# Causal attention of a decoder kernel: from the unit-pipelined stage with two score banks to the four-bank streamed stage

## What is computed

```python
n = layernorm(x[b])                         # no gain, no offset
q = n @ Wq; k = n @ Wk                      # Wq, Wk folded from a and b
v = n @ v_w.T + v_b
s = where(causal, q_h @ k_h.T, -inf) * 16 ** -0.5     # 16 heads, 112 x 112 each
x[b] += concat(softmax(s) @ v_h) @ o_w.T + o_b
```

## Time and profile before

| | us |
|---|---|
| median of 3 runs (lowest, highest) | 4157.95 (4157.94, 4166.34) |
| time of the profiled execution | 4158.94 |
| its span | 4157.2 |
| busy: TensorE, VectorE, ScalarE | 3770.2, 2553.9, 1778.3 |
| first instruction of the causal stage (its first memset) | 32.92 |
| first instruction of the next stage | 454.43 |

### The profile page before, as it was taken

The page is one execution under the profiler, slowest core; times in us unless marked ns, Lnnn a source line. Parts: engine busy times, 40 slices in busy tenths (PEclk is TensorE's granted clock), DMA queues, the critical chain, the costliest instruction groups (busy, mean ns, idle before and its releaser), DMA issues. The chain is left out here.

```text
span 4157.2 us, 85123 instructions
## 1 busy us (share of the span) xinstructions
PE 3770.2 (91%) x30568; PEld 2609.7 (63%) x30568; DVE 2553.9 (61%) x5295; ACT 1778.3 (43%) x4050; POOL 248.6 (6%) x453
## 2 busy tenths in 40 slices
PE   7999799999999879999778888886888799999999
PEld 6888555555555556677545556554666566666666
DVE  5777465665656557587656555553777556555555
ACT  4777455555555423244324434333777411111111
POOL 0000011111111100000000000000111000000000
PEclk9999999999999989999889999997999899999999
DMA  6000000000000000000033222222766500000000
GB/s 150 0 0 0 16 15 12 16 12 16 12 14 15 5 1 0 0 0 0 13 68 64 60 62 61 61 51 73 203 195 200 156 5 5 6 5 6 5 5 5
DMA packets 169129, 165.56 MB, mean 40 GB/s; under 512 B 96585, under 2 KB 157010, under 8 KB 168786
## 3 DMA queue, kind: packets, MB, share of 16 engines
q1 hardware_dynamic: 162912, 144.61, 13.5%
q10 hardware_dynamic: 6002, 17.89, 1.7%
HBM read 75.49 MB, written 55.05 MB: 31 GB/s over the span
## 5 line engine op out<-in xcount | busy, mean ns | idle before, releaser
L2388 DVE SCALAR_TENSOR_TENSOR g_residual<-m_out,m_gate,g_residual 112x256 f32 (+1 forms) x1280 | 549.2, 479 | 413.8 <-PE m_out L2232 406.5
L2232 PE MATMUL m_out<-e_down,m_hidden 128*112 128x256 f32 x2560 | 603.3, 379 | 0.0
L2232 PEld LDWEIGHTS m_out<-e_down,m_hidden 128*112 128x112 f32 x2560 | 452.5, 177 | 192.3 <-issue 110.8
L2221 PE MATMUL m_hidden_bank<-m_xT,e_up 128*128 128x448 f32 x1280 | 537.4, 545 | 3.2 <-issue 3.2
L2283 ACT ACTIVATE m_hidden<-m_hidden_bank 128x448 f32<-128x448 f32 x256 | 139.3, 544 | 646.5 <-PE m_hidden_bank L2221 646.5
L1705 DVE TENSOR_REDUCE x_top<-x_scores 112x4 f32<-112x1500 f32 x128 | 219.9, 1718 | 266.9 <-PE x_scores L1561 264.4
L2221 PEld LDWEIGHTS m_hidden_bank<-m_xT,e_up 128*128 128x128 f32 x1280 | 240.0, 191 | 149.7 <-issue 133.5
L1113 ACT ACTIVATE x_probs<-x_held,x_minus_top 112x488 f32<-112x488 f32 x256 | 177.5, 694 | 264.0 <-DVE x_minus_top L1169 264.0
L1024 PE MATMUL x_ring<-w_xkv,x_kv 128*122 128x512 f32 x512 | 233.4, 598 | 15.7 <-ACT x_k L822 15.0
L1017 PE MATMUL x_ring<-x_kv,w_xkv 128*128 128x488 f32 x512 | 240.4, 593 | 0.0
L1666 ACT ACTIVATE x_probsT<-x_scores 125x1792 f32<-125x1792 f32 x96 | 159.8, 1665 | 144.9 <-PE x_scores L1580 144.9
(11 more groups left out here) (288 smaller groups left out, 6769.0 us busy)
## 6 DMA issues: line engine op xcount, KB each, us to landing
by_position<-r_by_position SPq DMA_DIRECT2D x64, 784.0 KB, 4.2
r_bias<-by_position SPq DMA_DIRECT2D x64, 392.0 KB, 3.8
x_ctx<-in_ctx SPq DMA_DIRECT2D x64, 375.0 KB
x_kq_swapped<-x_kq_raw ACTq DMA_DIRECT2D x64, 243.5 KB, 3.6
x_slots<-x_kq SPq DMA_DIRECT2D x512, 30.4 KB
e_up<-in_L_ffn_keys SPq DMA_DIRECT2D x16, 256.0 KB, 5.8
e_down<-in_L_ffn_values SPq DMA_DIRECT2D x8, 512.0 KB, 6.6
g_residual<-in_x SPq DMA_DIRECT2D x4, 896.0 KB, 9.6
```

What stands on the lines that cost most here:

```text
L2221: ins = nc.tensor.matmul(hidden_bank[e % 2][:, 0:Q * T], M["up"][:, f, e, :], xT[par][:, f, :], start=(f == 0), stop=(f == DC - 1))
L2232: ins = nc.tensor.matmul(out_bank[2 * (e % 2) + i // 2][0:T, (i % 2) * D:(i % 2 + 1) * D], hidden[e % 2][:, i * T:(i + 1) * T], M["down"][ ...
L2388: nc.vector.scalar_tensor_tensor(row, out_bank[2 * (e % 2) + i // 2][0:T, (i % 2) * D:(i % 2 + 1) * D], gate[par][0:T, i, e:e + 1], row, A ...
```

## The change

`CausalAttention` is written anew as a `Streamed` stage on the driver `stream`. The methods `pe_probs`, `pe_paired` and `act_probs` are the bodies of pieces of `RelativeAttention`, moved into `Streamed` unchanged, and `RelativeAttention` calls them. The query is held twice, with even and odd heads masked; scores are matmuls over 32 partitions; one bound, one maximum, one subtraction and one exponential cover 16 heads. The sums come out of the value matmul's column of ones. The output weight is dense; the value bias is added at the copy of `onT`, and the output bias is added to the residual by a piece of its own, `bias`.

```diff
-for _name, _width in (("ident", P), ("mask8", 8), ("mask4", 4), ("row16", 1), ("parity", 2), ("keep0", T), ("keep1T", HS * T),
+for _name, _width in (("ident", P), ("mask8", 8), ("mask4", 4), ("row16", 1), ("parity", 2), ("keep0", HS * T), ("keep1T", HS * T),
...
-    put("keep0", np.where(causal, BIG, -BIG))
+    put("keep0", np.tile(np.where(causal, BIG, -BIG), (1, HS)))
...
-             wo=sb("wo", [P, HG, D]), vb=sb("vb", [P, D]),
+             wo=sb("wo", [P, DC, D]), vb=sb("vb", [P, DC]), ob=sb("ob", [P, D]),
...
-                     (W["vb"][:], t["L0_attn_v_b"].partition_broadcast(P))]
+                     (W["wo"][:], t["o_wT"].rearrange("(c p) n -> p c n", p=P)),
+                     (W["ob"][:], t["L0_attn_o_b"].partition_broadcast(P))]
+            loads += [(W["vb"][:, c:c + 1], t["L0_attn_v_b"].rearrange("(c p a) -> c p a", p=P, a=1)[c]) for c in range(DC)]
...
-            act.wait_ge(zeroed, 1)
-            for a in range(HS):
-                act.dma_start(W["wo"][SLOT * a:SLOT * a + HD, :, :], rows_in_slots(t["o_wT"])[a]).then_inc(copied, 16)
-                n += 16
-
-            act.dma_start(W["wo"][HD:HD + 1, 0, :], t["L0_attn_o_b"].rearrange("(a n) -> a n", a=1)).then_inc(copied, 16)
...
-            pool.memset(W["wo"][:], 0.0).then_inc(zeroed, 1)
...
-class CausalAttention(Phase):
...
+class CausalAttention(Streamed):
...
+        self.plan = Flow(4, [("stats", 0), ("scores", 2), ("f0", 3), ("k", 1), ("bound", 2), ("f1", 3), ("f2", 3), ("scale", 0),
+                             ("top", 2), ("f3", 3), ("bias", 0), ("less", 2), ("onT", 4), ("q", 1), ("heads", 3), ("xT", 0),
+                             ("v", 1), ("exp", 2), ("back", 3), ("project", 4)],
+                         bankless=("stats", "scale", "bias", "scores", "bound", "top", "less", "exp"))
...
+        self.xT = [sb(f"xT{i}", [P, DC, T]) for i in range(2)]
+        self.q = [sb(f"q{i}", [P, 2, DC, T]) for i in range(2)]
+        self.k = [sb(f"k{i}", [P, DC, T]) for i in range(2)]
+        self.v = [sb(f"v{i}", [P, H, SLOT]) for i in range(2)]
+        self.held, self.probs = sb("held", [P, H, T]), sb("probs", [P, H, T])
...
+        elif name == "scores":
+
+            self.ready_all(pe, ("q", "k"), b)
+            at_least(pe, self.bounded, b)
+            for f in range(DC):
+                for p in range(2):
+                    for j in range(HS):
+                        rows = slice(SLOT * j, SLOT * (j + 1))
+                        at = 512 * j + (2 * f + p) * T
+                        ins = nc.tensor.matmul(self.scores[0:T, at:at + T], self.q[par][rows, p, f, :], self.k[par][rows, f, :],
+                                               start=True, stop=True)
+            ins.then_inc(self.scored, 1)
+        elif name in ("f0", "f1", "f2", "f3"):
+            self.pe_probs(pe, name, b, c, body)
+        elif name == "heads":
+            self.pe_paired(pe, b, par, c, body)
...
+        elif name == "q":
+
+            bank = ring.take(act, c, body)
+            for p in range(2):
+                ins = nc.scalar.activation(self.q[par][:, p, :, :].rearrange("p f t -> p (f t)"), bank[:, 0:DC * T], ACT.Copy,
+                                           scale=self.const("parity")[:, p:p + 1])
+            ring.freed(ins, c)
...
+        elif name == "exp":
+            act.wait_ge(self.lessened, b + 1)
+            self.reuse(act, "f3", b)
+            nc.scalar.activation(self.probs[0:T, :, :], self.held[0:T, :, :], ACT.Exp, scale=self.scale).then_inc(self.exped, 1)
...
+        elif name == "onT":
+
+            bank = ring.take(act, c, body)
+            self.reuse(act, "project", b)
+            for f in range(DC):
+                ins = nc.scalar.activation(self.normedT[:, f, :], bank[:, f * T:(f + 1) * T], ACT.Identity,
+                                           bias=self.W["vb"][:, f:f + 1])
+            ring.freed(ins, c)
...
+        elif name == "bias":
+            nc.vector.tensor_tensor(X[0:T, b, :], X[0:T, b, :], self.W["ob"][0:T, :], ALU.add).then_inc(self.x_biased, 1)
+        elif name == "bound":
+            dve.wait_ge(self.scored, b + 1)
+            at_least(dve, self.exped, b)
+            nc.vector.scalar_tensor_tensor(
+                self.held[0:T, :, :].rearrange("t (j i) k -> t j (i k)", j=HS),
+                self.scores[0:T, :].rearrange("t (j c) -> t j c", c=512)[:, :, 0:4 * T], -BIG,
+                bc(self.const("keep0", T), 1, HS), ALU.max, ALU.min).then_inc(self.bounded, 1)
+        elif name == "top":
+            dve.wait_ge(self.bounded, b + 1)
+            nc.vector.tensor_reduce(self.tops[0:T, :], self.held[0:T, :, :], AX_X, ALU.max).then_inc(self.topped, 1)
+        elif name == "less":
+            dve.wait_ge(self.topped, b + 1)
+            nc.vector.tensor_tensor(self.held[0:T, :, :], self.held[0:T, :, :], bc(self.tops[0:T, :], 2, T),
+                                    ALU.subtract).then_inc(self.lessened, 1)
+        elif name == "back":
+            self.dve_back(dve, b, c, body, chain)
+        elif name == "project":
+            dve.wait_ge(self.x_biased, b + 1)
+            self.dve_project(dve, b, c, body)
```

More of the change, by code:

```diff
@@ L822, in copy_out @@
         self.ring.freed(self.nc.scalar.activation(dst, src_of(bank), ACT.Copy), c)
-class CausalAttention(Phase):
[L827 to L874, removed]
-        for a in range(HS):
-            h = HS * u + a
-            ins = self.nc.tensor.matmul(bank[0:T, a * T:(a + 1) * T], self.q[par][:, h // 8, h % 8, :],
-                                        self.k[par][:, h // 8, :], start=True, stop=True)
-        return ins
-    def act(self, act, name, b, par, c, body):
-        if name == "xT":
-            self.copy_out(act, c, body, self.xT[:].rearrange("p f t -> p (f t)"), lambda bank: bank[:, 0:DC * T])
-        elif name == "k":
-            self.copy_out(act, c, body, self.k[par][:].rearrange("p f t -> p (f t)"), lambda bank: bank[:, 0:DC * T])
-    def dve_bound(self, dve, u, par, b, hold, bank):
-        return self.nc.vector.scalar_tensor_tensor(hold, bank, -BIG, bc(self.const("keep0", T), 1, HS),
-                                                   ALU.max, ALU.min)
-    def dve(self, dve, name, b, par, c, body, chain):
-        nc, ring, X = self.nc, self.ring, self.X
-        if name == "stats":
-            self.norm_stats(self.norm, X[0:T, b, :], chain)
-        elif name == "scale":
-            self.reuse(dve, "xT", b)
-            self.norm_scale(dve, self.norm, b, self.xn[0:T, :], X[0:T, b, :]).then_inc(self.xn_ready, 1)
-        elif name == "q":
-            bank = ring.take(dve, c, body)
-            ring.freed(self.widen(self.q[par][:], bank[:, 0:DC * T], self.const("mask8"), DC, 8, T), c)
-        elif name == "v":
-            bank = ring.take(dve, c, body)
-            ring.freed(nc.vector.tensor_tensor(self.v[par][0:T, :, 0:HD],
-                                               bank[0:T, 0:D].rearrange("t (h d) -> t h d", h=H),
-                                               self.W["vb"][0:T, :].rearrange("t (h d) -> t h d", h=H), ALU.add), c)
-        else:
-            self.end_dve(dve, name, b, par, c, body)
@@ L1263, in pe_heads, with pe_probs, pe_paired, act_probs @@
         self.ring.filled(ins, c)
+    def pe_probs(self, pe, name, b, c, body):
+        j = int(name[1])
+        bank = self.ring.claim(pe, c, body)
+        pe.wait_ge(self.exped, b + 1)
+        for i in range(4):
+            ins = self.nc.tensor.transpose(bank[0:T, i * T:(i + 1) * T], self.probs[0:T, 4 * j + i, :],
+                                           self.const("ident", T)[:, 0:T])
+        self.ring.filled(ins, c)
+    def pe_paired(self, pe, b, par, c, body):
+        bank = self.ring.claim(pe, c, body)
+        self.ready_all(pe, ("v", "f0", "f1", "f2", "f3"), b, c)
+        for g in range(HG):
+            for a in range(HS):
+                h = HS * g + a
+                j, i = (h % 8) // 2, 2 * (h // 8) + h % 2
+                ins = self.nc.tensor.matmul(bank[SLOT * a:SLOT * (a + 1), g * T:(g + 1) * T], self.v[par][0:T, h, :],
+                                            self.probsT[0:T, j, i * T:(i + 1) * T], start=True, stop=True)
+        self.ring.filled(ins, c)
+    def act_probs(self, act, name, b, c, body):
+        j = int(name[1])
+        if j == 0:
+            self.reuse(act, "heads", b)
+        self.copy_out(act, c, body, self.probsT[0:T, j, :], lambda bank: bank[0:T, 0:4 * T])
     def pe_back(self, pe, b, c, body):
@@ L1923, in act @@
         elif name in ("f0", "f1", "f2", "f3"):
[L1924 to L1927 removed]
+            self.act_probs(act, name, b, c, body)
         elif name == "heads":
```

86 lines of the change are left out of this document (63 added, 23 removed).

## The result

| | before | after |
|---|---|---|
| median of the runs (lowest to highest), us | 4158.23 (4157.94 to 4166.34, 4 runs) | 4045.96 (4043.68 to 4048.34, 4 runs) |
| span of the profiled execution | 4157.2 | 4041.9 |
| busy in the span: TensorE, VectorE, ScalarE | 3770.2, 2553.9, 1778.3 | 3643.4, 2502.2, 1677.0 |
| last addition of the causal stage ends | 453.29 | 336.14 |

The ratio of the times is 0.9726, with a 95% interval of 0.9709 to 0.9742. The forecast was 4047.

A forecast was written before the change was run, and what follows sets the result against it. It took TensorE's instruction stream to bound the causal stage. Start 46 + 3, 31 frames of 8.8 and drain 20 end it at 341.8, 111.5 us less; with 0.5 for the prelude, 4047 us, range 4032 to 4074.

The forecast's parts named there:

- the prelude's 0.5: Prelude before the stages: loading a wider mask in the constants was taken to add 0.5 us.
- TensorE bound the stage before: Causal stage before the change: bound by TensorE's instruction stream, busy 39.02 of 40 us.
- TensorE's new frame, 8.49: New causal stage: TensorE's pieces for one batch, priced by their steps, sum to 8.49 us.
- VectorE's new frame, between 8.6 and 8.86: New causal stage: VectorE's operations for one batch sum to 8.86 us by full durations, 8.6 with overlaps.
- ScalarE, 7.5: New causal stage: ScalarE's work per batch is 7.5 us, hidden behind TensorE and VectorE.
- The single tiles, 8.8: Loop through the one `held` and one `probs`: bound to exponential to next bound, 8.8 us with hand-offs.
- The frame, 8.8: New causal stage: 8.8 us a batch, middle of VectorE's two ends plus a tenth of waiting; chance 0.50 for 8.5 to 9.0.
- The ends: Causal stage's start and drain: first bound at 46.0, slow early frames 3 us, drain 20.0, stage end 341.8.
- VectorE exposed (9.2): Rival, causal stage: VectorE binds with its waits exposed, 9.2 us a frame, time 4059; chance 0.25.
- TensorE waits for the exponential (9.63): Rival, causal stage: TensorE waits 1.14 us each frame at f0, 9.63 us a frame, time 4073; chance 0.18.
- The clock falls: Rival, causal stage: TensorE at its lower clock, 17.0 us a frame, time 4301, break-even 12.4; chance 0.03.
- No overlap (16.1): Rival, causal stage: single tiles make the engines' chains add, 16.1 us a frame, time 4273; chance 0.01.

The follow-up runs named there:

- e9: Kernel before, with half the contraction of query, key and value projections and two of four output matmuls left out; 4135.98 us against 4162.07, ratio 0.9938.
- e6: Changed kernel without the maximum and its subtraction, so the exponential takes the bounded scores; 4018.41 us.
- e8: Changed kernel with the masked queries of before and scores over 128 rows again; 4244.18 us, ratio 1.0201 to the kernel before.
- e10: Changed kernel with 96 more small 16x16 matmuls in TensorE's prelude, causal stage left alone; 4009.36 us.
- e1: Changed kernel with the output bias addition moved from VectorE to GpSimd; 4042.32 us.

## Why the prediction was right

The median was predicted 1 us too high (4047 for 4045.96), and that it came so near is in part luck. For the profiled execution the forecast was 4047.9, and it is 4043.68: the stage gained 5.65 more than was worked out, the measured end has the prelude's 0.5 already in it, and 117.15 - 115.3 = 1.85 was given back later, 5.65 + 0.5 - 1.85 = 4.3. The median lies 2.3 above that execution, where the forecast put it 1.0 below.

A second piece of luck is the term taken at nothing, that the other stages keep their time as they keep their instructions. The context stage took 800.1 us for 798.6. With 96 matmuls more in the new stage's unrolled frames it would have taken 762, and the whole some 4009, below the range.

- **TensorE bound the stage before.** Right, but thinly: e9 shows that other waits take over after 1 us a batch.
- **TensorE's new frame, 8.49.** It is 8.05 to 8.09. Scores (0.98), transposes of the probabilities (0.40 + 1.16 = 1.56 in the rows above), values (0.90), query (0.99) and output projection (0.96) came as priced. The difference lies in back, 0.44 for 0.53, in xT and onT, 0.25 and 0.19 for 0.29 each, and in key and value projection, 0.90 and 0.86 for 0.99 and 0.96.
- **VectorE's new frame, between 8.6 and 8.86.** It is 8.37, below the lower end. Each operation has the duration that was taken; eight times in a frame neighbours overlap, by 0.05 to 0.09 each. The lower end allowed for too few of these overlaps. This is the mis-sized term.
- **ScalarE, 7.5.** It is busy 30.08 of 40 us, 6.5 a frame; hidden, as was said.
- **The single tiles, 8.8.** This loop was priced too high for the same overlaps: from the bound at 202.86 to the end of the exponential at 211.14 it is 8.28, with a hand-off 8.4. It is not what binds: a second `held` changed nothing (e2). What I called "a few tenths" behind the addition is the closing piece of the loop that does bind, together with TensorE's wait at f0. The prediction compared three cycles and left out this fourth, which runs through both engines over two frames.
- **The frame, 8.8.** 8.60 measured, 6 us less in 31 frames; the middle of a wrong interval plus a tenth came near the loop's 8.62.
- **The ends.** The first bound came at 47.15 (46.0), the slow early frames cost some 0.4 us (3; five frames, to the bound at 90.59, take 43.4 us, where five steady ones take 43.1), the drain took 22.3 (20.0). The last bound came at 313.8 (322). The end of the stage was predicted 5.7 us too late (341.8 against 336.14).
- **VectorE exposed (9.2).** Its mechanism is there in a small dose: VectorE is the fullest engine, and waits for the projection, 0.49 us in every other frame. The price of 8.86 + 0.35 was too high on both terms. VectorE is busy 38.34 of 40 us, and e6 shows that it holds the frame by 0.6 us only. The rule cited for this rival, of the Trainium skill, TensorEngine Tiling (Array Packing), section PSUM Bottleneck, is on emptying PSUM. In this trace only bound, reciprocal, scaling and the residual addition read PSUM, 2.02 + 0.25 + 0.42 + 0.41 = 3.1 of VectorE's 8.37 us, so that VectorE is full agrees with the rule's outcome but does not show its cause.
- **TensorE waits for the exponential (9.63).** By the sign I had given, f0 idling by over 0.5 us, this rival would have won: f0 idles 0.77 us, in every other frame. In part it did, since that idling is TensorE's side of the two-frame loop: 8.09 + 0.52 is the frame. Both of its terms were too high (8.49 and 1.14), and the sign did not tell it from the forecast. The waits for the exponential sum to 15.0 us in 29 frames.
- **The clock falls.** It did not: 1.00 while TensorE idles 0.28 and 0.77 us in turn, behind a ring of four banks. With stands of 3 us a frame (e8) it was granted 0.87, and that kernel is slower than the one before. So the clock can fall, at a much larger idling than here; e8 takes 14.9 us a frame, above the break-even of 12.4, but most of that is its waits and not the clock. The working took a projection at the lower level for twice the upper, by setting a duration (1.91 us at 39.23) beside a step (0.99); as durations they are 1.91 and 1.15, so 2 x 8.49 was an upper end.
- **No overlap (16.1).** Nothing of it was seen.

## What to carry to other kernels

When two engines are nearly level, look for a loop that goes through both over two frames: frame times that alternate (8.37, 8.86) are a first sign of it, and the cure was to move what stands behind the last wait. It is a sign only: VectorE's bounds in e6 alternate too (7.76 and 8.34), and there TensorE is simply full. Follow the chain before believing it. The work of an addition between two dependent operations was partly free (0.22 us for 0.42). Scores in row groups pay in full only when neighbouring matmuls are in different groups (0.98 us for 2.42). Look at which engine empties a ring bank, and at what stands ahead of that in its list. Compare the untouched stages of two kernels too: one of them may have moved for a reason that is not in the edit.

## What the runs showed that I had not expected

- A loop's place in TensorE's program is worth 38 us of 800 in an untouched stage (761, 800 or 826 us), by stands of 3.3 to 4.1 us once a turn and slower matmuls behind each. The profile names a DMA for them, though all three lengths have the same DMA and e10 does not stand.
- A single row group of 32 partitions costs 2.42 us for 32 records of 112 columns, 128 partitions 3.5, four groups in turn 0.98.
- A ring bank that is emptied late by VectorE cost 3.0 us of TensorE a frame, and with it the clock: 0.87.
- GpSimd adds 112x256 in 0.73 us (e1), where VectorE takes 0.42; VectorE's maximum beside it still takes 2.01.
